# Another semaphore wait ahead of the quantizing of hq in the down projection of a transformer layer on eight cores

## The reference

```python
def _act_quant(x):
    scale = 127.0 / jnp.clip(jnp.max(jnp.abs(x), axis=-1, keepdims=True), 1e-05)
    xq = jnp.clip(jnp.round(x * scale), -128.0, 127.0) / scale
    return x + jax.lax.stop_gradient(xq - x)

def _bitlinear(x, w):
    return jnp.einsum('bsi,oi->bso', _act_quant(x), _weight_quant(w))
gate = jax.nn.silu(_bitlinear(x, w_gate))
up = _bitlinear(x, w_up)
return _bitlinear(gate * up, w_down)      # inner size 4096, output 1024

x = _layernorm(x + _L0_attn_ref(x, ...), axis=-1)
x = _layernorm(x + _L0_ffn_ref(x, ...), axis=-1)
```

## Time and profile before

| | us |
|---|---|
| median of 2 runs | 3931.01 (3928.3 to 3933.72) |
| profiled execution, its own time | 3933.39 |
| span of its slowest core | 3931.8 |
| spans of the eight cores | 3908.2 to 3931.8 |

### The profile page before, as it was taken

One profiled execution on the slowest core, in us unless ns is written; L12 is line 12 of the kernel. 1 busy time (PEld: TensorE's weight loads), 2 busy tenths in 40 slices (PEclk: granted clock), 3 DMA queues, 4 the chain that ended last, 5 costly groups with the idle time before them and its releaser, 6 DMA issues.

```text
span 3931.8 us, 32057 instructions; the slowest of 8 cores (3908.2 to 3931.8 us)
## 1 busy us (share of the span) xinstructions
PE 1829.5 (47%) x8824; PEld 614.2 (16%) x8824; DVE 1509.7 (38%) x2965; ACT 976.6 (25%) x1164; POOL 18.7 (0%) x54
## 2 busy tenths in 40 slices
PE   1201212221044444566766883765295529453854
PEld 0000001000011111111111110322142214121321
DVE  1453464444445544322122113443434244414433
ACT  1202102220000024565866882110011002001100
POOL 1000000000000000000000000000000000000000
PEclk9998555555556555555555555876697769676967
DMA  5445443322400000000000001411151124022312
GB/s 115 158 160 183 157 157 92 79 59 95 158 16 9 1 11 17 28 12 32 1 17 27 1 1 60 133 59 41 67 163 38 56 91 132 27 78 92 104 35 70
DMA packets 140980, 278.38 MB, mean 71 GB/s; under 512 B 7944, under 2 KB 106504, under 8 KB 134664
## 3 DMA queue, kind: packets, MB, share of 16 engines
q1 hardware_dynamic: 107256, 192.96, 14.8%
q10 hardware_dynamic: 24320, 67.12, 4.9%
q0 software_dynamic: 9232, 16.25, 2.6%
HBM read 250.61 MB, written 41.94 MB: 74 GB/s over the span
## 4 chain that ended last, share of the span: by engine, by line
PE 23%; DVE 15%; ACT 14%; issue 5%; DMA 5%; DVEq 1%; ACTq 0%; SPq 0%
PE ps_f L1174 7%; PE ps_f L1062 6%; PE ps_f L1068 6%; ACT PTb L730 3%; ACT PTb L734 3%; ACT PT L730 3%; ACT PT L734 3%; DMA wdbuf<-scr_d 2%; PE ps_tf L958 2%; DMA xo_t<-xo 2%; DVE hq L1134 1%; DVE den_sb L808 1%; DVE hbuf L1126 1%; DVE hbuf L1130 1%; PE ps_sc L706 1%
## 5 line engine op out<-in xcount | busy, mean ns | idle before, releaser
L706 PE MATMUL ps_sc<-qn,khat 32*128 32x512 bf16 (+3 forms) x1280 | 313.3, 532 | 134.6 <-ACT PT L730 48.2
L1174 PE MATMUL ps_f<-wdbuf,hqT 128*128 128x512 bf16 x1024 | 314.7, 471 | 85.4 <-DMA wdbuf<-scr_d 36.4
L1062 PE MATMUL ps_f<-wgbuf,xqT 128*128 128x512 bf16 x1024 | 248.6, 387 | 113.8 <-DMA wubuf<-scr_u 112.9
L1068 PE MATMUL ps_f<-wubuf,xqT 128*128 128x512 bf16 x1024 | 243.8, 381 | 0.0
L742 DVE TENSOR_TENSOR PT<-PT,maskD 128x512 bf16<-128x512 bf16 x64 | 27.2, 425 | 489.0 <-ACT PT L734 489.0
L1082 DVE SCALAR_TENSOR_TENSOR hbuf<-ps_f,xsc,gate_s 128x512 f32<-128x512 f32 x128 | 96.1, 751 | 266.8 <-ACT gate_s L1076 266.8
L730 ACT ACTIVATE PT<-ps_sc,negMb 128x1024 bf16<-128x1024 f32 (+3 forms) x160 | 157.8, 986 | 121.2 <-PE ps_sc L706 108.8
L958 PE MATMUL ps_tf<-ident,hq 128*128 128x128 bf16 x512 | 66.8, 275 | 258.8 <-DVE hq L1134 258.8
L353 PE MATMUL ps_tr<-ident,xst 128*128 128x128 bf16 x384 | 52.2, 304 | 269.5 <-DVE xTc L29 179.7
L1076 ACT ACTIVATE gate_s<-ps_f,xsc 128x512 f32<-128x512 f32 x128 | 88.0, 687 | 345.2 <-PE ps_f L1068 345.2
L730 ACT ACTIVATE PTb<-ps_sc,negMb 128x1024 bf16<-128x1024 f32 (+3 forms) x160 | 157.8, 986 | 36.0 <-PE ps_sc L706 24.6
(11 more groups left out here) (226 smaller groups left out, 2485.7 us busy)
## 6 DMA issues: line engine op xcount, KB each, us to landing
wgbuf<-scr_g SPq DMA_DIRECT2D x32, 1024.0 KB, 6.2
wubuf<-scr_u SPq DMA_DIRECT2D x32, 1024.0 KB, 9.2
wfbuf<-wgT SPq DMA_DIRECT2D x8, 2048.0 KB, 10.0
wfbuf<-wgT ACTq DMA_DIRECT2D x8, 2048.0 KB, 8.5
wfbuf<-wuT SPq DMA_DIRECT2D x8, 2048.0 KB, 13.2
wfbuf<-wuT ACTq DMA_DIRECT2D x8, 2048.0 KB, 9.9
wfbuf<-wdT SPq DMA_DIRECT2D x32, 512.0 KB, 3.9
wfbuf<-wdT ACTq DMA_DIRECT2D x32, 512.0 KB, 4.2
```

Source lines behind the costliest of these rows:

```text
L706: e.matmul(ps_sc[:, j * 512 + stc:j * 512 + 512], khat[32 * j:32 * j + 32, gi * T + sc * 128: gi * T + sc * 128 + 128], qn[32 * j:32 * j + 32,
L1062: P.emit(t, lambda e, c=c, i4=i4, bi=bi, gb=gb: e.matmul(ps_f[:, gb:gb + 512], xqT[:, i4 * D + c * 128:i4 * D + c * 128 + 128], wgbuf[bi][ ...
L1068: P.emit(t, lambda e, c=c, i4=i4, bi=bi, ub=ub: e.matmul(ps_f[:, ub:ub + 512], xqT[:, i4 * D + c * 128:i4 * D + c * 128 + 128], wubuf[bi][ ...
L1174: e.matmul(ps_f[:, ((2 + i4) % 4) * 512: ((2 + i4) % 4) * 512 + 512], hqT[:, i4 * INNER + io * 128: i4 * INNER + io * 128 + 128], wdbuf[bi ...
```

## The change

VectorE's third quantizing step writes the quarter i4 of hq. Until now it waited for everything given to TensorE so far. Now it waits for the transposes that last read this same quarter, one b8 before (or in the chunk before), and for nothing on the first use. `mk_tr4` keeps that mark for each i4; it is taken after `ftr_batch`, when cT.v counts the four transposes just emitted. Nothing else is touched: same instructions, order and buffers.

```diff
                                       ew, b)
                     return mk_scl
 
+                mk_tr4 = [None, None, None, None]
                 if STAGE >= 5:
                     mk_scl = emit_xprep(0)
                 for tc in range(4 if STAGE >= 5 else 0):
@@ -1134,7 +1135,8 @@
                                                    e.tensor_scalar_max(
                                                        hq[:, i4 * 512:i4 * 512 + 512],
                                                        hbuf[:, hs:hs + 512], -128.0),
-                                                   waits=[(cT, cT.v)],
+                                                   waits=([mk_tr4[i4]]
+                                                          if mk_tr4[i4] else []),
                                                    incs=[(cV, 1)])
                                     srcs = [hq[:, i4 * 512 + k * 128:
                                                i4 * 512 + k * 128 + 128]
@@ -1145,6 +1147,7 @@
                                                       i4 * INNER + b8 * 512 + 512],
                                                   psl[:, 0:512]))(i4, b8),
                                               [(cV, mk_hq[1])], i4 % 2)
+                                    mk_tr4[i4] = (cT, cT.v)
```

## The result

The changed kernel takes 3889.8 us in the median (3885.1 to 3895.6, 7 runs), the kernel before 3932.2 on the same chip (3928.3 to 3933.7, 6 runs): a ratio of 0.9893, with a 95% interval of 0.9881 to 0.9905. That is 42 us less, faster and clear of noise but within 2%. Forecast were 3898, with a range of 3885 to 3915. With an interval of 0.12% to each side, the measurement tells much less than 2% from no change, other than the prediction thought.

What follows compares the result with a forecast made beforehand. No engine or transfer bounds fh=0, but a chain passing from engine to engine. The wait's 28.8 us and shorter matmul groups' 3.8 us make 32.6 us less, from the 3931.01 median to 3898 us, range 3885 to 3915.

Steps and rivals of the forecast that it cites:

- The place: First half of the down projection (fh=0), L1134 at i4=0, b8 1 to 7: 28 waits, 182.9 us, would go.
- the other 100 waits: L1134's remaining waits, at i4=1 to 3: covered by DVE's own L1126 and L1130, so nothing won or lost.
- The wait's term: End of matmuls to copy L29 at i4=0: 1.42 us falls to 0.39, saving 1.03 us, 28 times: 28.8 us.
- The page's rule on transposes: Skill page says the fast clock doesn't engage for transposes: set behind matmuls 0.58 us, saving 0.83; prediction kept 0.38 and 1.03.
- rival 5: Slow transposes behind the matmuls at i4=0: the set takes 0.58 us, saving 27.0 us, 3904 us; chance 0.05.
- The group term: Groups of 16 down-projection matmuls shorten with the gap, 0.13 us per us: 3.8 us less over 28.
- The sum: Whole kernel: 28.8 + 3.8 = 32.6 us less, 3898 us from the median 3931.01.
- Where the idle time went: DVE's idle at L1134 moves to L29, growing some 150 us; PE's before first transposes, b8 1 to 7, 0.86 to 0.
- Rival 1: DVE runs far ahead, quantizing all four quarters under the matmuls: 207 us less, 3724 us; chance 0.01.
- Rivals 2 and 3: First transposes still held, only L1134's 0.43 us saved each: 3919, chance 0.05; or wait hidden by another, no effect: 3931, chance 0.05.
- Rival 4: Matmul groups stay at the low clock to their end, 6.99 us each: 4.5 us slower, 3935.5 us; chance 0.05.

Runs made afterwards that it cites:

- the fastest kernel: Changed kernel with all hqT copies on ScalarE and four wdbuf buffers instead of two, all issued by SyncE's queue: 3632.2 us against 3941.9, ratio 0.9212.

## Why the prediction was right, point by point

- **The place.** Right. The 182.9 us of waits are gone, all of the gain comes with i4=0, and the other 100 waits are worth nothing; both were run apart.
- **The wait's term, 1.03 us a turn.** From the end of the matmuls to L29 it is 0.40 us where 0.39 was worked out, so the 0.17 us of overlap taken from gate/up holds here too: 1.42 - 0.40 = 1.02. The gap as a whole shrank by 1.12 (10.08 to 8.96), 31 us and not 28.8. The rest is a step that the prediction didn't have: the set of i4=2, whose end releases a copy on DVE's path, now begins 4.4 us behind the matmuls and not 5.4, and often still runs at the high clock. In the turn above it took 0.38 us (3787.08). Of the 200 turns with complete records it did so in 133, in the kernel before in 2 of 200. The gap is 8.78 us in such turns, in the median, and 8.96 in most others. The prediction named a set as cover only.
- **The page's rule on transposes.** The first set behind the matmuls took 0.38 or 0.39 us in all 28 cases of core 5. As before, sets of transposes run at either clock (0.38 and 0.58 us), so rival 5 did not come about. "TensorE: Matmul & The Clock Gate" of the Trainium skill, Part 4, says that the fast clock doesn't engage for transpose mode; the 0.38 us don't bear this out for transposes that follow matmuls. Whether transposes by themselves would raise the clock, no run here tests.
- **The group term, 0.14 us shorter each, 3.8 us.** This is the term that was mis-sized: groups are 5.43 for 5.73, 0.30 each, 8.4 us. Its working was wrong in kind as well. It read a slope from groups behind gaps of 0.97, 5.17 and 9.97 us, as if length rose evenly with the gap. The runs don't show that: 4.62 at 3.16, 6.12 at 7.40, 5.43 at 8.96, 5.63 at 9.37, 5.57 at 9.84, 5.73 at 10.08, 5.96 at 10.91. From 8.96 on the length rises, 0.5 us in 2 us of gap; the point at 7.40 breaks the line by far more than the scatter, though that kernel also has other engines at work inside the gap. The groups of one stretch show more. Those of the fence above began with a low-clock part of 5.5, 3.8, 3.3 and 2.9 us (matmuls 0.43 us apart, then 0.22), then 5.8: at turns of 14.1 to 15.4 us the rise comes a little earlier in each group, until it jumps back. In the earlier trace rows, at turns of 15.0 to 16.7, it comes later in each: 2.9, 5.0 and 5.9, then 2.9 again. In the kernel before with the copies on ScalarE it doesn't move: in one stretch of core 7 six turns in a row took 13.65 to 13.69 us, the rise came 5.8 us into each group, and each took 6.36 or 6.37 us. So the length goes with how the whole turn fits to the moments at which the clock rises. That is read from these rows and explains the long groups at 7.40; no run was made to test it. That the slope got the sign right is luck. What held was to carry the term with wide ends, 4.89 and 6.57.
- **The sum.** Terms of 31 and 8 make 39.5 us (28 x 1.41 of the turns); 42.4 were measured. The 3 us that are left lie in no term and are smaller than the difference between runs of one kernel. The mean span of the eight cores in the two profiled executions fell by 40.7 us (3920.7 to 3880.0), which is nearer to the sum.
- **Where the idle time went.** L29's grew by 141 us, forecast were some 150; groups shorter by 0.30 leave DVE 28 x 0.30 = 8.4 us less to wait. PE's idle time ahead of the transposes of i4=0 fell as forecast, from 24.5 us to none. In all it fell by 20.8 only, since ahead of the other sets it grew by some 3: the sets before them end sooner, those of i4=1 and 2 with 12.1 and 12.8 us for 14.0 and 16.4.
- **Rival 1** was rightly ruled out by DVE's order, and priced at 207 us. With its condition made true, the copies off DVE, it came: 169 us between the kernels with and without the narrow wait. **Rivals 2 and 3** are refuted by the 0.40 us. **Rival 4** has a real mechanism: in the kernel before with the copies on ScalarE longer groups took back 0.39 us a turn. But they never took all, and no mean group came near 6.83.

## What to carry to other kernels

A wait that is too wide costs only what its engine could have done before the next thing it must wait for in its own order: here one step of twelve. Look for the instruction that blocks next (here a copy on the same engine) before pricing a narrower wait, and move that as well: the two edits together were worth 240 us, apart 42 and 71. Where an engine's clock rises inside each burst of work, carry a term for the burst's length with ends from the rows, and don't interpolate it: here a shorter gap made bursts longer once (6.12 us at 7.40).

## What the runs showed of the hardware that was not expected

- The mean length of the same 16 matmuls doesn't simply grow with the time between groups: 3.94 to 6.12 us over the kernels here, and 6.12 stand behind a gap of 7.40 where 5.43 stand behind 8.96. What seems to count is whether the rise of the clock comes at the same place in each turn: at turns of 13.66 us it stayed 5.8 us into the group, turn after turn. The granted clock of the changed kernel's last such stretch was 0.68 (core 5), before 0.64 (core 1):

```profile
3690.00:3811.00 121.00, 58.45 (x256) 25.20 (x256) 51.33 (x124) 9.39 (x16) 0.00 (x0) 0.68 0.12 35
```

- In the fastest kernel most turns take 6.73 us, with 3.1 us from group to group that four sets of transposes partly fill, and from the second group on nearly all stay at the high clock: 3.61 us, 37% less than the 5.73 of before.
- A VectorE memset of 128x1 behind another costs 0.195 us from start to start (four in 0.78; each runs for 0.06), less than the 0.26 of the small steps L1108 to L1114.
